# Edge sums: the first eight blocks are gathered in step with VectorE

## The reference, cut to what matters

```
e     = leaky_relu(a1[src] + a2[dst], 0.2)          # one number per edge and head
m     = segment_max(e, dst);  ex = exp(e - m[dst])
alpha = ex / segment_sum(ex, dst)
out   = segment_sum(ft[src] * alpha[:, :, None], dst)
```

## Time and profile before

| | us |
|---|---|
| median of 3 timed runs | 1890.13 |
| lowest, highest | 1889.97, 1891.54 |
| span of the profiled execution (its own time is recorded as this span only) | 2276.6 |
| edge sums es0 in it | 684.0 |
| edge sums es1 in it | 757.5 |
| all else in it | 835.1 |

### The profile page before, as it was taken

One profiled execution on the slowest core, in us unless ns is written; L12 is line 12 of the kernel. 1 busy time (PEld: TensorE's weight loads), 2 busy tenths in 40 slices (PEclk: granted clock), 3 DMA queues, 4 the chain that ended last, 5 costly groups with the idle time before them and its releaser, 6 DMA issues. The chain is left out here.

```text
span 2276.6 us, 34460 instructions
## 1 busy us (share of the span) xinstructions
PE 1646.4 (72%) x9468; PEld 1342.0 (59%) x9468; DVE 1163.6 (51%) x3309; ACT 656.1 (29%) x2160; POOL 1009.6 (44%) x1093
## 2 busy tenths in 40 slices
PE   5177776677778978999463665777577777689991
PEld 4045555556656557999343554555455556689991
DVE  7256566555456664222452555556566657841223
ACT  4222121122322554333152222332222212643330
POOL 4556555656543002555124545555454541325550
PEclk9588888889889989999786777888787989599996
DMA  7323222333222016666532222222222220267666
GB/s 167 98 71 84 80 75 75 87 82 87 78 70 58 1 63 224 211 213 210 135 112 72 80 74 77 74 80 75 70 77 68 72 72 20 93 199 213 215 202 178
DMA packets 148002, 244.24 MB, mean 107 GB/s; under 512 B 53369, under 2 KB 83368, under 8 KB 147558
## 3 DMA queue, kind: packets, MB, share of 16 engines
q0 software_dynamic: 48384, 134.19, 21.1%
q1 hardware_dynamic: 97306, 106.27, 15.7%
q10 hardware_dynamic: 2124, 1.54, 0.3%
HBM read 210.48 MB, written 31.21 MB: 106 GB/s over the span
## 5 line engine op out<-in xcount | busy, mean ns | idle before, releaser
L679 POOL DMA_INDIRECT es_rows<-table,eall x784 | 745.7, 951 | 719.3 <-SPq L668 418.6
L699 PE MATMUL bank<-es_msg,es_one 128*125 128x264 f32 x976 | 305.3, 466 | 123.5 <-DVE es_msg L822 104.1
L699 PE MATMUL bank<-es_rows,es_won 128*125 x976 | 289.8, 448 | 116.8 <-DVE es_won L819 84.8
L762 ACT ACTIVATE es_oneT<-bank 125x512 bf16<-125x512 f32 x244 | 145.1, 595 | 755.9 <-remote 488.5
L699 PEld LDWEIGHTS bank<-es_msg,es_one 128*125 128x125 f32 x976 | 209.0, 225 | 175.2 <-DVE es_msg L822 113.9
L699 PEld LDWEIGHTS bank<-es_rows,es_won 128*125 128x125 f32 x976 | 202.4, 218 | 159.2 <-issue 125.3
L842 DVE TENSOR_TENSOR es_z<-es_rows,es_near 128x4 f32<-128x4 f32 (+1 forms) x244 | 43.1, 177 | 359.3 <-ACTq L774 265.2
L1237 PE MATMUL bank<-ffn_xbT,ffn_w 128*128 128x128 f32 x1792 | 220.8, 277 | 0.0
L1290 ACT ACTIVATE xT<-bank,ffn_b1s 128x128 f32<-128x128 f32 x448 | 128.2, 369 | 303.2 <-PE bank L1237 292.6
L1396 DVE TENSOR_TENSOR xT<-bank,xT 128x256 f32<-128x256 f32 x112 | 47.6, 425 | 327.8 <-issue 190.1
L1247 PE MATMUL bank<-ffn_w,xT 128*128 x896 | 211.7, 379 | 0.0
(11 more groups left out here) (445 smaller groups left out, 2408.8 us busy)
## 6 DMA issues: line engine op xcount, KB each, us to landing
ffn_w<-in_L_ffn_W SPq DMA_DIRECT2D x112, 512.0 KB
es_rows<-table,eall POOLq DMA_INDIRECT x784
ffn_w<-yrows SPq DMA_DIRECT2D x20, 560.0 KB
ffn_w<-in_L_ffn_W SPq DMA_DIRECT2D x2, 4096.0 KB
xrows<-acc SPq DMA_DIRECT2D x10, 560.0 KB
table<-acc SPq DMA_DIRECT2D x5, 577.5 KB
table<-acc SPq DMA_DIRECT2D x5, 564.4 KB
out_x<-xs SPq DMA_DIRECT2D x5, 560.0 KB
```

The lines of the kernel that those rows point to most:

```text
L679: pool.indirect_dma_start(rows[:, q % R, w, :], None, m.table[H], bass.IndirectOffsetOnAxis(ap=m.eall[:, at:at + 1], axis=0)).then_inc(gat ...
L699: ins = pe.matmul(sum_banks[p % 2][0:P, 0:W], left, right, start=(w == 0), stop=(w == BW - 1))
L762: a.activation(oneT[:, p % 2, :], turn_bank[0:P, :], ACT.Copy).then_inc(kept, 1)
```

## The change

GpSimd still gathers blocks 0 and 1 at once. Each of blocks 2 to 7 now waits until `zed` has reached q - 1, that is until VectorE's small operations of step q - 2 are done. The branch on the flag moves from ahead of block 8 to ahead of block 2. Blocks from 8 on wait for `freed` as before. Both calls of `edge_sums` change. No instruction is added on any other engine.

```diff
     LATE = 4
     OWN = 5
+    AHEAD = 2
...
                 for q in range(NBLK):
-                    if q == R:
+                    if q == AHEAD:
                         bounds.gpsimd(pool)
                     if q >= R:
                         pool.wait_ge(freed, q - R + 1)
+                    elif q >= AHEAD:
+                        pool.wait_ge(zed, q - AHEAD + 1)
                     for w in range(BW):
                         at = (q * BW + w) * 2
                         pool.indirect_dma_start(rows[:, q % R, w, :], None, m.table[H],
```

## The result

| | before | after | ratio [95%] |
|---|---|---|---|
| median us (4 runs each) | 1890.84 | 1904.89 | 1.007 [1.0056, 1.0085] |
| span of the profiled execution, us | 2276.6 | 1903.2 | |

The change makes the kernel slower, by 14.05 us between the medians and 10.6 to 16.1 by the interval (1890.84 x 0.0056 and x 0.0085). The forecast's 27.3 us had the right sign and about twice the size.

The account below looks back on a forecast made before the run. The prediction took GpSimd's issue of gathers to bound both edge-sum stages in timed runs. First waits of 9.2 us (es0) and 18.1 us (es1), all else 0, add 27.3 to 1890.1: 1917 us, with an 8-in-10 range of 1884 to 1926.

Parts of the forecast that it names:

- The limit, from 93% of a stage worked out: Both edge-sum stages: gathers take GpSimd 982 of 1055 us in the timed run, so its issue is the limit or near it.
- the whole 386.5 us: Profiled span beyond the timed median, all put into the two edge-sum stages, leaving 1055 us for them when timed.
- The branch: 0: Flag load and jump on GpSimd, moved into the wait for step 0: no cost; about 1 us a stage without cover.
- The first wait in es0: 9.2: Start of es0: GpSimd stands still from 78.1 to 87.3 until step 0's small operations end, 9.2 us.
- The first wait in es1: 18.1: Start of es1: GpSimd stands still 18.1 to 21.1 us until step 0's small operations end; lower end taken.
- The other five waits: 0: Blocks 3 to 7 of each stage: step q - 2 is always done before block q - 1 is issued, no cost.
- Nothing makes the delay up: they are the limit to the end of the stage.: Gathers behind GpSimd's waiting instruction in both stages: delay stays to the stage's end, so all 27.3 us count.
- The span to stay near 2277: Profiled execution after the change: its span stays near 2277 us or shrinks by up to 46 us.
- The rule beside the second rival: GpSimd's track, not solid with DMA slices, would not be the limit: time stays at 1890 us; second rival's chance 0.19.
- The real flood: Rival: gathers at the stages' starts starve other engines in timed runs too; 1843 to 1892, half way 1868 us; chance 0.17.
- Longer stops: Rival, both stages' first waits: 13 + 21.1 + 2 for the branches, 36 us, 1926 us; no separate chance given.
- the gathers don't bind: Second rival, both stages: a timed gather takes only 0.949 us, steps are the limit, 1890 us; no-change chance 0.19.

Follow-up runs that it names:

- e_null: The changed program with the order of before (eight blocks at once in both stages), against the kernel before: 1890.97 us, ratio 0.9998.
- e_mid1: The order of before plus one added wait ahead of block 42 in es1, against the kernel before: 1900.93 us, ratio 1.0054.
- e_one: The changed kernel with one block at once, block q waiting for step q - 1, against the kernel before: 1956.16 us, ratio 1.0356.
- e_first: The changed kernel with only the wait ahead of block 2 kept in each stage, against the kernel before: 1910.72 us, ratio 1.0099.
- e_two: The changed kernel itself run again on another chip, against the kernel before: 1908.38 us, ratio 1.0104.
- e_es0b: The waits in es0 only, run again on the second chip, against the kernel before: 1896.08 us, ratio 1.0034.
- e_es0: The waits in es0 only, eight blocks at once in es1, against the kernel before: 1896.63 us, ratio 1.0031.
- e_four: Four blocks at once in both stages, then block q after step q - 4, against the kernel before: 1894.76 us, ratio 1.0013.
- e_mid0: The order of before plus one added wait ahead of block 42 in es0, against the kernel before: 1890.37 us, ratio 1.0004.
- e_es1: The waits in es1 only, eight blocks at once in es0, against the kernel before: 1905.33 us, ratio 1.0078.

## Why the prediction was right in its sign and twice too large

**The limit, from 93% of a stage worked out.** For es1 right: of e_null's 527.0 us there GpSimd's gathers take 495.4 from the first start to the last (1511.2 - 1015.8), GpSimd waits 5.1 us for slots in all, and e_mid1 and e_one pass their stops on. For es0 it was wrong: see below. Putting the whole 386.5 us into the edge sums was right, as the sums' line of before shows (L699, es0 and es1):

```profile
L699 PE MATMUL bank<-es_rows,es_won x976: 378/382/792, 115.0 to 744.1; 128*125 x196
...
L699 PE MATMUL bank<-es_msg,es_one x976: 386/386/804, 1231.0 to 1932.2; 128*125 128x264 f32 x196
```

From the first gather to the last sum that is 676.2 (744.1 - 67.9) and 756.1 us (1932.2 - 1176.1), together 1432.3; e_null has 518.6 + 527.0 = 1045.6. The 386.7 between them are nearly all of the 389.0 between the spans (2276.6 - 1887.6).

**The branch: 0.** No run took it apart. GpSimd's restarts follow L851's ends by 0.28 us (86.03 - 85.75 and 1045.64 - 1045.36), so nothing of it shows.

**The first wait in es0: 9.2.** 8.8 measured, 8.5 without the usual gap. Step 0's L845 starts 17.7 us behind the first gather (84.99 - 67.3); the forecast had 18.7 (86.56 - 67.9).

**The first wait in es1: 18.1.** 15.6 measured, 15.3 without the gap: this term was too large by 2.5 to 2.8. The forecast took its durations from the stretch in which the trace of before was disturbed. All seven groups of L2068 take 4.46 us in a row (1034.71 to 1039.17), 19.1 us behind the first gather where the forecast had 20.3. From L765 to the end of L851 it is 6.0 us (1039.37 to 1045.36), where the trace of before had 7.40. The reason for taking the lower end of 18.1 to 21.1, that es1 would make a part of a longer stop up because its steps are nearer to the gathers' pace, was the wrong way round: es1 makes nearly nothing up.

**The other five waits: 0.** Right, by e_first.

**"Nothing makes the delay up: they are the limit to the end of the stage."** This is the step that failed, for es0. There GpSimd is not the limit to the end: in e_null it waits for slots ten times, 16.8 us in all, 15.2 of it between 240 and 320 us, so it has time to give. The stop of 8.5 us costs es0 5.0. Where those 5.0 are lost the first eleven small operations show, with VectorE's idle time ahead of them, in e_null and then in after, with three of after one by one:

```profile
L845 DVE TENSOR_TENSOR es_z<-es_rows,es_near x11: 153/162/214, 85.3 to 124.4; 128x4 f32<-128x4 f32 x11
...
  ACTq L777: 7.1, 7
```

```profile
L845 DVE TENSOR_TENSOR es_z<-es_rows,es_near x11: 156/164/165, 85.0 to 129.7; 128x4 f32<-128x4 f32 x11
...
  ACTq L777: 12.6, 9
...
108.17 0.16 DVE L845 TENSOR_TENSOR es_z<-es_rows,es_near 128x4 f32<-128x4 f32 x1 [2.13 <-ACTq L777]
113.28 0.16 DVE L845 TENSOR_TENSOR es_z<-es_rows,es_near 128x4 f32<-128x4 f32 x1 [1.45 <-ACTq L777]
118.60 0.16 DVE L845 TENSOR_TENSOR es_z<-es_rows,es_near 128x4 f32<-128x4 f32 x1 [2.54 <-ACTq L777]
```

Ten steps take 39.1 us with eight blocks in hand and 44.7 with two, and the waits for `ready` (L777) account for 5.5 of the 5.6 us between them. In the middle the steps go at the gathers' 5.1 to 5.3 us, each waiting for `ready`, as the forecast said, but only these first ones, and the 5 us stay to the end.

One pair of profiles would be weak evidence, since es0's way scatters by several us. But at the start ten profiles, all but e_one's, agree. In the five with the wait in es0 (after, e_two, e_es0b, e_es0, e_first) VectorE waits 12.0 to 12.6 us for `ready` in its first eleven steps, and the eleventh small operation starts 61.5 to 62.4 us behind the first gather. In the five without a stop at that place (e_null, e_four, e_mid0, e_mid1, e_es1) it waits 7.1 to 8.0, and the operation starts at 56.6 to 57.9.

The forecast had the steps at 3.93 us catching up with the gathers for good. It left out that the 122 steps of a stage share 98 blocks, so that further on a step needs less than one block, and in es0 GpSimd gets ahead again until the ring is full. The section on the kernel says that the first 19 or so steps have a block each and all belong to the first tile; the table of steps in fact takes blocks of the two halves of the edge list in turn, so that some early steps already share a block. The rest of the stop, 3.5 us, comes out of the stock of blocks: from the 15th step to the last after's small operations stay 5.0 to 5.4 us later than e_null's (counted from the first gather), while its gathers are 8.6 to 9.7 us later from block 12 to block 36 and 5.1 to 5.4 from block 41 on. GpSimd gets the difference back where e_null waits for slots. In the five profiles with the wait block 36 is issued 9.1 to 10.0 us later than in e_null and block 48 only 4.1 to 6.6.

So the sum reads 5.0 for es0, not 9.2, and 13.4 for es1, not 18.1: 18.4 between the profiles of e_null and after. The timed runs measured 13 to 20 for the whole change. They alone would not settle es0: e_es0 and e_es0b cost 5.9 [2.6, 8.9] and 6.4 us [3.0, 10.0] by the ratio, and 8.5 lies inside both intervals. That it loses less than its stop is read from the profiles and from e_mid0.

**The span to stay near 2277.** It fell to 1903.2, for a reason that has nothing to do with the change. Holding the holes for a matter of that execution alone was right; expecting the next profile to have them was not consistent with it.

**The rivals.** The real flood falls by e_null. Longer stops fall by the measured ones. That the gathers don't bind falls for es1 and holds in part for es0. The rule beside the second rival (the Trainium skill, Perfetto Trace Analysis, section What "DMA-bound" means) reads a limit from a track that is solid with DMA slices. The window of es1 in e_null (columns as above):

```profile
1015.00:1545.50 530.50, 428.88 (x2758) 350.17 (x2758) 435.27 (x1093) 186.28 (x700) 372.81 (x392) 0.95 0.38 101
```

The gathers fill 372.8 of 530.5 us, 70%, while VectorE's work fills 435.3 and TensorE's 428.9, and GpSimd was still the limit. What the track doesn't show as busy is the 0.30 us between any two gathers: 391 of them are 117 us.

## What to carry to other kernels

A queue that issues at a steady pace with steady gaps can be the limit at 70% busy: compare pace times count with the stage's length, and look whether its engine ever waits for a free slot. Where it hardly did (es1), a stop cost nearly its full length, at the start (13.4 of 15.3 us) and in the middle (11.7 of 12.0). Where it did wait for slots (es0), a stop cost only what the consumers were starved of: nothing with a full ring behind it, and a good half at the stage's start, where the stock wasn't built yet. And when the profiled execution is far longer than the timed one, take no duration from its disturbed stretches; the same order profiled again is worth more than any argument on it.

## What the runs showed of the hardware

- One profiled execution of the same order of instructions took 2276.6 us and another 1887.6; nearly all of the difference lay in the edge sums, with ScalarE idle for 18.39 us at a stretch though its input was there. None of the eleven later profiles shows it. What it was stays open.
- GpSimd's indirect DMA of 128 rows kept its pace of 1.25 us (a median of 0.946 and a gap of 0.30) in both stages of the eleven later profiles, and eight blocks of it in a row did not delay the first step: 17.7 us behind the first gather in e_null and in after.
- At the start of es0, where after has fewer sums in the same stretch, TensorE's mean granted clock is lower too: 0.83 in after and 0.93 in e_null, 1 being the upper of its two levels (2.4 GHz). The windows of 86.3 to 126 us in e_null and then in after, busy times for L702 alone (stretch, busy us of PE and PEld, granted clock, DMA share, GB/s). What part the clock has in the loss of that stretch was not taken apart; behind it, from the 15th step to the last, the two profiles differ by 5.0 to 5.4 us throughout.

```profile
86.30:126.00 39.70, 21.41 (x80) 15.29 (x80) 0.93 0.39 106
```

```profile
86.30:126.00 39.70, 19.75 (x66) 13.84 (x67) 0.83 0.38 104
```

- es0's way scatters more than es1's between profiles with the same order there: 517.6 to 527.0 us in five (e_null, e_four, e_mid0, e_mid1, e_es1), and 525.4 to 528.0 in four of es1 (e_es0, e_null, e_mid0, e_es0b). The two longest of the five, 521.8 and 527.0, have the lowest clock, 0.912. The scatter comes late: from the 45th small operation to the last the three profiles with a clock of 0.912 (these two and e_es0) take 3.3 to 6.7 us longer than e_null, the other seven at most 0.4 more or less. Whether the clock is the cause was not tested.
